# The six middle rounds in TensorE's program: a loop over pairs of rounds, or written out

## The chip, the cores and the metric

The kernel runs on one core of a Trainium2 chip. The metric is the device time of one launch in microseconds (us), as the median of several runs.

## What is computed

There are 4096 rows of 1024 numbers: 64 samples of 64 rows each. Two layers are added to `x`, one after the other. Cut to what matters:

```python
# layer 0: a 64x64 matrix for each sample mixes the sample's rows
y   = einsum('bct,bcd->bdt', x, weights0[cond])
h   = einsum('bnd,erd->bner', y, A0);  route = top-2 softmax of y @ W_gate.T
x   = x + (y @ W_base.T + b_base) + einsum('bner,eor->bno', h * route, B0)
# layer 1: a 1024x1024 adapter for each sample, then low rank
z   = einsum('bsi,boi->bso', x, weight1[adapter])
out = x + 2 * einsum('bshr,hor,bsh->bso', z @ A1, B1, 8 * softmax(z @ Wr.T + br))
```

Everything is float32. The kernel reaches nearly that accuracy by splitting both factors of a product into a high and a low part and adding three products.

## The kernel before

**Preparation.** In the first 84 us TensorE folds the adapter matrices of layer 1 with `A1` and `Wr` into matrices of 1024 x 136 (`fold`), with one turn of a loop for each adapter that is in use. They go to a DRAM buffer `folded`. The first rows are mixed (`mix`).

**Rounds.** After that the work goes in eight rounds (`ROUNDS = 8`) of 512 rows. In round r TensorE's program (`iteration`, lines 404 to 443) does layer 0 of round r, layer 1 of round r-1 and the mixing of round r+1:

- `gates` (L349, L351): 64 products, alternating 272 and 136 columns, into `mix_ps`, `low_ps` and `out_ps`.
- eight steps of `base` (L316 to L318, 12 products of 512 columns each), and after each step a `make_low` (L384, 8 products of 272 columns) for one sample of round r-1. `make_low` number i waits until the matrix of that sample has landed in slot i % 3 of `adapter`.
- `delta`, eight more steps of `base` with `mix` (L336) and `make_out` between them, `delta` again, and a last `make_out`.

TensorE executes in program order. Round 0 stands by itself, then come rounds 1 to 6, then round 7, whose second half of rows has code of its own. Rounds 1 to 6 are a loop of three turns with two rounds in each turn (L459 to L461):

```python
with pe.Fori(0, (ROUNDS - 2) // 2) as q:
    for r in (1, 2):
        iteration(q, r)
```

So turn 0 is rounds 1 and 2, turn 1 is rounds 3 and 4, turn 2 is rounds 5 and 6, and the program branches back twice: before round 3 and before round 5. In the loop, the value that a semaphore must reach is worked out from `q` in a register (`at`).

**The other engines** have the same loop of pairs in programs of their own, and the change leaves these alone. In each round, SyncE issues the loads of the next round's `x_rows` and `wc` (L236, L243), the two loads of 1 MB into `xT` (L254), and then the stores of the round before (L261), in this order. GpSimd loads the folded matrix of one sample (1.1 MB, L869) into a slot of `adapter` as soon as TensorE's `make_low` three samples before has finished with that slot (`low_done`). VectorE and ScalarE split and copy what TensorE has made.

Of the kernel before, what the change touches and what calls it, by code (L numbers as in the profile page):

```python
# [24 lines left out]
ROUNDS = TOKENS // T  # L25
# [20 lines left out]
def build(nc, x, x_turned, cond_ids, adapter_ids, w_cond, w0, g0, bias, b0, w1, ag1, b1, br, folded, out):  # L46
    with ExitStack() as ctx:
# [152 lines left out]
        def at(q, r, per, n=0):  # L200

            return 2 * per * q + (per * r + n)
# [111 lines left out]
        def _(pe):  # L314
# [14 lines left out]
            def mix(q, r, k):  # L329
                if k == 0:  # L330
                    pe.wait_ge(x_landed, at(q, r, 16 * TILES, 16 * TILES))
                    pe.wait_ge(wc_landed, at(q, r, 16 * PER, 16 * PER))
                if k >= 2:
                    pe.wait_ge(yT_lo_done, at(q, r, KC, k - 1))
                for t in range(TILES):
                    mm = pe.matmul(mix_ps[k % 2][:, t * P:(t + 1) * P], x_rows[:, t, k * P:(k + 1) * P], wc[:, t, :],  # L336
                                   start=True, stop=True, skip_group_check=True)
                mm.then_inc(yT_done, 1)

            def gates(q, r):  # L340
                for t in range(TILES):
                    tile = slice(t * P, (t + 1) * P)
                    if t >= 2 and (r >= 1 or not isinstance(q, int)):
                        pe.wait_ge(final_done, at(q, r - 2, KC, 2 * KC - 1 + t - 2))
                    for k in range(KC):
                        if t == 0 and k in (0, KC - 1):

                            pe.wait_ge(yT_lo_done, at(q, r, KC, KC - 1 if k == 0 else KC))
                        pe.matmul(hg_banks[t][:, 0:2 * HG], yT[:, 0, k, tile], g_hl[:, k, :, :].rearrange("p h n -> p (h n)"),  # L349
                                  start=(k == 0), stop=False, skip_group_check=True)  # L350
                        mm = pe.matmul(hg_banks[t][:, 0:HG], yT[:, 1, k, tile], g_hl[:, k, 0, :],  # L351
                                       start=False, stop=(k == KC - 1), skip_group_check=True)
                    mm.then_inc(hg_done, 1)

            def base(q, r, half, k, toks=ALL):
                bank = ALL if toks == ALL else A
                for n in range(4):
                    if k == 0:

                        if half == 1:  # L360
                            pe.wait_ge(x1_done, at(q, r + (toks == B), KC, n + 1))
                        elif toks == B:
                            pe.wait_ge(x1_done, at(q, r, KC, HALF + n + 1))
                        elif half == 0 and (r >= 1 or not isinstance(q, int)):
                            pe.wait_ge(x1_done, at(q, r - 1, KC, HALF + n + 1))
                    cols = slice((HALF * half + n) * P, (HALF * half + n + 1) * P)
                    product(base_ps[n][:, bank], w_hi[:, k, cols], w_lo[:, k, cols], yT[:, 0, k, toks],
                            yT[:, 1, k, toks], k == 0, False)

            def delta(half, toks=ALL):  # L370
                bank = ALL if toks == ALL else A
                for n in range(4):
                    cols = slice((HALF * half + n) * P, (HALF * half + n + 1) * P)
                    product(base_ps[n][:, bank], b0_hi[:, cols], b0_lo[:, cols], hwT[:, 0, toks], hwT[:, 1, toks],
                            False, True).then_inc(main_done, 1)

            def make_low(q, r, i, banks):
                pe.wait_ge(adapter_landed[i % SLOTS], 16 * at(q, r, (3, 3, 2)[i % SLOTS], i // SLOTS + 1))
                pe.wait_ge(x1T_lo_done, at(q, r, 2 * PER, 2 * i + 2))
                if i >= 2:  # L380
                    pe.wait_ge(lg_done, at(q, r, PER, i - 1))
                bank = banks[i % 2]
                for k in range(KC):
                    mm = pe.matmul(bank[:, 0:2 * HG], x1T[:, i % 2, k, :, :].rearrange("p h n -> p (h n)"),  # L384
                                   adapter[:, i % SLOTS, k, :, :].rearrange("p h n -> p (h n)"),
                                   start=(k == 0), stop=(k == KC - 1))
                mm.then_inc(low_done, 1)

            def turn_hw(q, r):
                pe.wait_ge(route_step, at(q, r, ROUTE_STEPS, ROUTE_STEPS))  # L390
                for t in range(TILES):
                    mm = pe.transpose(mix_ps[0][:, t * P:(t + 1) * P], rows[:, t, :], identity[:, :])
                mm.then_inc(hwT_done, 1)

            def turn_lw(q, r, tiles=range(TILES)):
                pe.wait_ge(score_step, at(q, r, SCORE_STEPS, SCORE_STEPS))
                for t in tiles:
                    mm = pe.transpose(low_ps[:, t * P:(t + 1) * P], rows[:, t, :], identity[:, :])
                mm.then_inc(lwT_done, 1)

            def make_out(q, r, n, bank, free, toks=ALL):
                if n == 0:
                    pe.wait_ge(lwT_lo_done, at(q, r, 1, 1))
                if free:
                    pe.wait_ge(final_done, at(q, r, KC, KC + free))
                cols = slice(n * P, (n + 1) * P)
                product(bank, b1_hi[:, cols], b1_lo[:, cols], lwT[:, 0, toks], lwT[:, 1, toks], True, True
                        ).then_inc(out_done, 1)

            def iteration(q, r, l1=True, ahead=True, toks=ALL):  # L410
                first = isinstance(q, int) and r == 0
                if first:
                    pe.wait_ge(g_split, 1)
                gates(q, r)
                for k in range(KC):
                    if first:
                        pe.wait_ge(side_lo, 1 + k)
                    base(q, r, 0, k, toks)
                    if l1:
                        if k < 2:  # L420
                            pe.wait_ge(hg_copied, at(q, r, TILES, TILES))
                        make_low(q, r - 1, k, low_banks)
                    if k == 5:
                        turn_hw(q, r)
                pe.wait_ge(hwT_lo_done, at(q, r, 1, 1))
                if first:
                    pe.wait_ge(side_lo, B0_SPLIT)
                delta(0, toks)
                for k in range(KC):
                    if first:  # L430
                        pe.wait_ge(side_lo, HALF1 + k // 2 + 1)
                    base(q, r, 1, k, toks)
                    if ahead:
                        mix(q, r + 1, k)
                    if l1 and k == 1:
                        turn_lw(q, r - 1)
                    if l1 and k >= 2:
                        make_out(q, r - 1, k - 2, out_ps[:, :], k - 2)
                if l1:
                    make_out(q, r - 1, KC - 2, low_ps[:, :], 0)  # L440
                delta(1, toks)
                if l1:
                    make_out(q, r - 1, KC - 1, out_ps[:, :], KC - 2)
# [12 lines left out]
                mix(0, 0, k)  # L456
            iteration(0, 0, l1=False)
            pe.wait_ge(side_lo, SIDES)
            with pe.Fori(0, (ROUNDS - 2) // 2) as q:  # L459
                for r in (1, 2):  # L460
                    iteration(q, r)  # L461
            last = ROUNDS - 1
            iteration(0, last, ahead=False, toks=A)

            for k in range(KC):
# [481 lines left out]
```

## Time and profile before

| | |
|---|---|
| median of 3 runs | 754.27 us (751.4 to 755.64) |
| the profiled execution: its own time | 755.48 us |
| its span in the profile | 753.8 us |
| TensorE busy | 723.9 us, 96% of the span |
| VectorE, ScalarE, GpSimd busy | 339.9, 113.6 and 57.9 us |
| DMA engines | mean 207 GB/s |

The profiled execution has its own time of 755.48 us beside a span of 753.8 us; 1.7 us lie around the span. "Idle" of an engine is the time between the end of one of its instructions and the start of the next. Matmuls overlap and their ends are modelled, so a distance from start to start is also used. The rounds begin with the first product of `gates`, at 160.75, 239.57, 320.16, 401.25, 482.58, 563.65 and 642.93 us for rounds 1 to 7. PEclk is the granted clock of TensorE, 1.00 for 2.4 GHz and 0.50 for 1.2 GHz.

### The profile page before, as it was taken

Reading aid. Unit: us, or ns where it says so; the run is one execution under the profiler, and the core shown is the slowest. Engines: PE = TensorE matmul, PEld = TensorE weight load, DVE = VectorE, ACT = ScalarE, POOL = GpSimd, SP = SyncE. Lnnn points to the kernel's source line nnn. Section 1 sums busy time; section 2 is a strip of 40 time slices with the busy share of each in tenths; the row PEclk is TensorE's granted clock in tenths of the full one; section 3 lists DMA queues with packets and bytes.
Section 4 is the critical chain, followed back from the end, with each engine's and each line's share of the span. In section 5 each row is a group of like instructions: output and inputs, shape, how many; then the busy total and the mean of one; then the engine's idle time right before and its main releaser. Section 6 shows DMA issues by size and latency. Waiting matters only on the chain.

```text
span 753.8 us, 12433 instructions
## 1 busy us (share of the span) xinstructions
PE 723.9 (96%) x4424; PEld 646.1 (86%) x4424; DVE 339.9 (45%) x900; ACT 113.6 (15%) x309; POOL 57.9 (8%) x115
## 2 busy tenths in 40 slices
PE   8999899999999999999999999899999999989984
PEld 8999887898888888797889888888889888989983
DVE  2000295145625553455426452455345443764544
ACT  1222300112111111101111211111111111111110
POOL 1222300001000110001000100011000000010100
PEclk9999999999999999999999999999999999999996
DMA  7899992038603882178514951467218831793622
GB/s 279 324 415 377 399 395 87 1 118 343 242 32 116 311 294 98 57 244 312 178 57 173 394 193 48 170 266 266 98 57 289 311 133 56 257 338 155 242 76 95
DMA packets 38708, 156.30 MB, mean 207 GB/s; under 512 B 8836, under 2 KB 11908, under 8 KB 28420
## 3 DMA queue, kind: packets, MB, share of 16 engines
q1 hardware_dynamic: 27714, 78.72, 28.0%
q0 software_dynamic: 9216, 71.31, 25.8%
q10 hardware_dynamic: 1730, 5.58, 1.8%
q8 instruction: 36, 0.59, 0.3%
q14 instruction: 12, 0.10, 0.0%
HBM read 133.24 MB, written 22.35 MB: 206 GB/s over the span
## 4 chain that ended last, share of the span: by engine, by line
PE 86%; DMA 5%; DVE 4%; issue 2%; SPq 2%; ACT 0%; POOLq 0%; DVEq 0%
PE base_ps L316 16%; PE base_ps L317 16%; PE base_ps L318 16%; PE base_ps L325 8%; PE mix_ps L336 7%; DMA adapter<-folded 4%; PE low_ps L384 4%; PE out_ps L384 4%; PE mix_ps L349 3%; PE out_ps L316 2%; PE out_ps L317 2%; PE out_ps L318 2%; DVE w_lo L629 1%; PE low_ps L349 1%; PE out_ps L349 1%
## 5 line engine op out<-in xcount | busy, mean ns | idle before, releaser
L316 PE MATMUL base_ps<-yT,w_hi 128*128 128x512 f32 (+1 forms) x576 | 214.5, 372 | 1.3 <-DVE xT L749 1.1
L318 PE MATMUL base_ps<-yT,w_hi 128*128 128x512 f32 (+1 forms) x576 | 211.5, 367 | 0.0
L317 PE MATMUL base_ps<-yT,w_lo 128*128 128x512 f32 (+1 forms) x576 | 211.4, 367 | 0.0
L633 DVE TENSOR_TENSOR yT<-mix_ps,yT 128x512 fp32r<-128x512 f32 x64 | 44.2, 691 | 240.0 <-ACT yT L515 239.8
L316 PEld LDWEIGHTS base_ps<-yT,w_hi 128*128 128x128 f32 x576 | 108.5, 188 | 20.8 <-DVE xT L749 4.0
L318 PEld LDWEIGHTS base_ps<-yT,w_hi 128*128 128x128 f32 x576 | 108.5, 188 | 18.1
L317 PEld LDWEIGHTS base_ps<-yT,w_lo 128*128 128x128 f32 x576 | 108.6, 188 | 15.5
L869 POOL DMA_DIRECT2D adapter<-folded x64 | 34.1, 532 | 606.2 <-PE low_ps L384 505.9
L645 DVE TENSOR_TENSOR x1T<-xT,x1T 128x256 fp32r<-128x256 f32 x128 | 48.3, 419 | 66.6 <-ACT x1T L523 66.6
L325 PE MATMUL base_ps<-ag_raw,stage 128*128 128x136 f32 x640 | 74.7, 279 | 2.3 <-issue 1.3
L325 PEld LDWEIGHTS base_ps<-ag_raw,stage 128*128 128x128 f32 x640 | 74.3, 190 | 2.8 <-issue 1.5
L523 ACT CAST x1T<-xT 128x256 fp32r<-128x256 f32 x128 | 44.7, 403 | 189.1 <-PE low_ps L384 63.6
L336 PEld LDWEIGHTS mix_ps<-wc,x_rows 128*128 128x128 f32 x512 | 66.0, 191 | 7.3 <-DVE yT L633 2.2
L515 ACT CAST yT<-mix_ps 128x512 fp32r<-128x512 f32 x64 | 37.5, 587 | 213.6 <-PE mix_ps L336 213.6
L336 PE MATMUL mix_ps<-wc,x_rows 128*128 128x128 f32 x512 | 67.1, 275 | 2.1 <-DVE yT L633 1.6
L749 DVE SCALAR_TENSOR_TENSOR xT<-base_ps,bias_cols,xT 128x512 f32<-128x512 f32 (+1 forms) x72 | 44.7, 683 | 8.0 <-PE base_ps L318 7.8
L755 DVE TENSOR_TENSOR xT<-xT,out_ps 128x512 f32<-128x512 f32 (+1 forms) x53 | 34.9, 659 | 9.2 <-PE out_ps L318 9.2
L384 PEld LDWEIGHTS low_ps<-adapter,x1T 128*128 128x128 f32 x240 | 33.0, 188 | 6.3 <-issue 3.1
L384 PE MATMUL low_ps<-adapter,x1T 128*128 128x272 f32 x240 | 35.2, 289 | 3.2 <-DMA adapter<-folded 3.2
L349 PE MATMUL mix_ps<-g_hl,yT 128*128 128x272 f32 x128 | 32.6, 346 | 4.1 <-issue 3.5
L384 PEld LDWEIGHTS out_ps<-adapter,x1T 128*128 128x128 f32 x240 | 33.2, 188 | 2.8 <-DVE lg L699 0.6
L384 PE MATMUL out_ps<-adapter,x1T 128*128 128x272 f32 x240 | 35.1, 288 | 0.2 <-DMA adapter<-folded 0.2
(126 smaller groups left out, 724.2 us busy)
## 6 DMA issues: line engine op xcount, KB each, us to landing
adapter<-folded POOLq DMA_DIRECT2D x64, 1088.0 KB, 7.0
stage<-in_w SPq DMA_DIRECT2D x40, 512.0 KB, 7.9
x_rows<-in_x SPq DMA_DIRECT2D x32, 512.0 KB, 6.0
xT<-in_x_turned SPq DMA_DIRECT2D x16, 1024.0 KB, 7.2
out<-xT SPq DMA_DIRECT2D x28, 512.0 KB, 2.7
folded<-adapter ACTq DMA_DIRECT2D x10, 544.0 KB, 6.9
w_raw<-in_w SPq DMA_DIRECT2D x8, 256.0 KB, 8.1
w_raw<-in_w SPq DMA_DIRECT2D x4, 512.0 KB, 12.0
```

The source lines that it names most:

```text
L316: pe.matmul(dst, st_hi, mv_lo, start=start, stop=False, skip_group_check=True)
L317: pe.matmul(dst, st_lo, mv_hi, start=False, stop=False, skip_group_check=True)
L318: return pe.matmul(dst, st_hi, mv_hi, start=False, stop=stop, skip_group_check=True)
L325: mm = pe.matmul(base_ps[c % BANKS][:, 0:HG], stage[:, c, oc * P:(oc + 1) * P], ag1_raw[:, oc, :], start=(oc == 0), stop=(oc == KC - 1))
L336: mm = pe.matmul(mix_ps[k % 2][:, t * P:(t + 1) * P], x_rows[:, t, k * P:(k + 1) * P], wc[:, t, :], start=True, stop=True, skip_group_chec ...
L349: pe.matmul(hg_banks[t][:, 0:2 * HG], yT[:, 0, k, tile], g_hl[:, k, :, :].rearrange("p h n -> p (h n)"), start=(k == 0), stop=False, skip_ ...
L384: mm = pe.matmul(bank[:, 0:2 * HG], x1T[:, i % 2, k, :, :].rearrange("p h n -> p (h n)"), adapter[:, i % SLOTS, k, :, :].rearrange("p h n ...
L515: act.copy(yT[:, 0, k, :], mix_ps[k % 2][:, :]).then_inc(yT_hi_done, 1)
L523: act.copy(x1T[:, i % 2, p * HALF:(p + 1) * HALF, 0, :], xT[:, half_of(r, p), :, i * CH:(i + 1) * CH]).then_inc(x1T_hi_done, 1)
L633: dve.tensor_tensor(yT[:, 1, k, :], mix_ps[k % 2][:, :], yT[:, 0, k, :], ALU.subtract).then_inc(yT_lo_done, 1)
L645: dve.tensor_tensor(x1T[:, i % 2, half, 1, :], xT[:, half_of(r, p), :, i * CH:(i + 1) * CH], x1T[:, i % 2, half, 0, :], ALU.subtract).then ...
L749: dve.scalar_tensor_tensor(row, base_ps[n % HALF][:, bank], bias_cols[:, n:n + 1], row, ALU.add, ALU.add).then_inc(x1_done, 1)
```

## The change

TensorE's loop over pairs of rounds is gone. A Python loop calls `iteration` for rounds 1 to 6 with `q = 0`, so that all six stand one behind the other in TensorE's program:

```diff
             pe.wait_ge(side_lo, SIDES)
-            with pe.Fori(0, (ROUNDS - 2) // 2) as q:
-                for r in (1, 2):
-                    iteration(q, r)
             last = ROUNDS - 1
+            for r in range(1, last):
+                iteration(0, r)
             iteration(0, last, ahead=False, toks=A)
```

The matrix products, their order and their operands stay as they are. The values that semaphores must reach are now constants. The programs of the other four engines are unchanged.

On TensorE, at the entry of the loop (end of round 0, start of round 1), the program was:

```order
L318 MATMUL base_ps<-hwT,b_hi 128x512
L459 UNCONDITIONAL_BRANCH
L459 ISA
L349 MATMUL mix_ps<-g_hl,yT 128x272
L351 MATMUL mix_ps<-g_hl,yT 128x136
```

The branch and the register instruction at L459 are gone; the first product of round 1 now follows the last one of round 0 directly.

On TensorE, at the end of the loop's body, before:

```order
L316 MATMUL out_ps<-lwT,b_hi 128x512
L317 MATMUL out_ps<-lwT,b_lo 128x512
L318 MATMUL out_ps<-lwT,b_hi 128x512
L459 REGISTER_ALU
L459 COMPARE_AND_BRANCH
L349 MATMUL mix_ps<-g_hl,yT 128x272
L351 MATMUL mix_ps<-g_hl,yT 128x136
```

and at the end of round 2 now:

```order
L316 MATMUL out_ps<-lwT,b_hi 128x512
L317 MATMUL out_ps<-lwT,b_lo 128x512
L318 MATMUL out_ps<-lwT,b_hi 128x512
L349 MATMUL mix_ps<-g_hl,yT 128x272
L351 MATMUL mix_ps<-g_hl,yT 128x136
```

In the first listing the branch goes back to the start of round 1's code for rounds 3 and 5, and the products below it are those of round 7. In the second the products below are those of round 3; nothing stands between the rounds. TensorE's written program grows from 1616 such rows to 2834, and 51 of its 59 register operations are gone.

## Rows read from the trace of the kernel before

**Rows 1.** The page, its busy times (TensorE) and its DMA queues (instruction fetches).
```profile
PE 723.9 (96%) x4424; PEld 646.1 (86%) x4424; DVE 339.9 (45%) x900; ACT 113.6 (15%) x309; POOL 57.9 (8%) x115
...
q8 instruction: 36, 0.59, 0.3%
```

**Rows 2.** TensorE's waits from 160 to 645 us: total, times, longest.
```profile
PE mix_ps L349 <- issue: 3.5, 2, 1.9
PE low_ps L384 <- DMA adapter<-folded: 1.9, 3, 1.5
PE mix_ps L351 <- issue: 0.2, 1, 0.2
```

**Rows 3.** Timeline of TensorE, round 1 into 2: start, duration, instruction.
```profile
239.34 0.39 PE L318 MATMUL out_ps<-lwT,b_hi 128*128 128x512 f32 x1
239.57 0.28 PE L349 MATMUL mix_ps<-g_hl,yT 128*128 128x272 f32 x1
```

**Rows 4.** The same, at the two branches back (rounds 2 into 3, 4 into 5).
```profile
318.15 0.39 PE L318 MATMUL out_ps<-lwT,b_hi 128*128 128x512 f32 x1
320.16 0.39 PE L349 MATMUL mix_ps<-g_hl,yT 128*128 128x272 f32 x1 [1.63 <-issue]
...
323.29 0.34 PE L349 MATMUL mix_ps<-g_hl,yT 128*128 128x272 f32 x1
323.85 0.22 PE L351 MATMUL mix_ps<-g_hl,yT 128*128 128x136 f32 x1 [0.22 <-issue]
...
480.28 0.39 PE L318 MATMUL out_ps<-lwT,b_hi 128*128 128x512 f32 x1
482.58 0.39 PE L349 MATMUL mix_ps<-g_hl,yT 128*128 128x272 f32 x1 [1.91 <-issue]
```

**Rows 5.** Instruction queue in the DMA view of 316.5 to 317, then 480 to 480.5.
```profile
q8 instruction: 1, 0.02, 21.2%
...
q8 instruction: 1, 0.02, 12.0%
```

**Rows 6.** Instruction queue in the DMA view of the whole round 1, then round 3.
```profile
q8 instruction: 4, 0.07, 0.3%
...
q8 instruction: 5, 0.08, 0.4%
```

**Rows 7.** Busy times by stretch, rounds 1, 3, 4, 5; third from last: granted clock.
```profile
160.75:239.57 78.82, 78.79 (x442) 68.48 (x440) 39.28 (x104) 11.72 (x28) 4.23 (x8) 1.00 0.50 183
...
320.16:401.25 81.09, 79.34 (x440) 68.62 (x441) 37.87 (x101) 10.59 (x25) 4.23 (x8) 1.00 0.53 190
401.25:480.28 79.03, 78.80 (x440) 68.23 (x439) 38.81 (x102) 11.71 (x28) 4.24 (x8) 1.00 0.53 194
482.58:563.65 81.07, 80.82 (x441) 70.15 (x441) 37.88 (x101) 10.39 (x24) 4.24 (x8) 0.98 0.52 190
```

**Rows 8.** The same view around the second branch back, and after the first.
```profile
482.00:484.00 2.00, 1.42 (x11) 1.43 (x12) 0.00 (x0) 0.50 (x2) 0.00 (x0) 0.98 0.69 266
484.00:486.00 2.00, 2.00 (x11) 2.00 (x11) 0.75 (x3) 0.00 (x0) 0.00 (x0) 0.50 0.91 324
486.00:488.00 2.00, 2.00 (x13) 2.00 (x13) 0.36 (x2) 0.00 (x0) 0.00 (x0) 0.66 1.07 313
...
322.00:324.00 2.00, 1.78 (x16) 1.68 (x16) 1.11 (x3) 0.00 (x0) 0.00 (x0) 1.00 0.92 279
```

**Rows 9.** Timeline of TensorE, `make_low` that waited, rounds 3 and 4.
```profile
347.66 0.39 PE L384 MATMUL low_ps<-adapter,x1T 128*128 128x272 f32 x1 [1.49 <-DMA adapter<-folded]
...
426.97 0.36 PE L384 MATMUL low_ps<-adapter,x1T 128*128 128x272 f32 x1 [0.20 <-DMA adapter<-folded]
```

**Rows 10.** Round 3: SyncE's `xT` loads, then the chain of waits.
```profile
334.89 0.87 SPq L254 DMA_DIRECT2D xT<-in_x_turned  x2
...
336.51 10.93 DMA adapter<-folded
```

**Rows 11.** Round 4: SyncE's `xT` loads, GpSimd's adapter load and its landing.
```profile
416.31 0.90 SPq L254 DMA_DIRECT2D xT<-in_x_turned  x2
...
417.11 0.54 POOL L869 DMA_DIRECT2D adapter<-folded  x1 [3.22 <-PE out_ps L384]
...
DMA to landing us min/median/max: 9.6/9.6/9.6
```

## The prediction, made before the changed kernel was run

> **What bounds the kernel now.** I read the busy times first: TensorE works for 723.9 us, 96% of the span, and no other engine comes to half of it [rows 1]. So only what TensorE executes and where it stands still counts. Next I read its waits over rounds 1 to 6, the stretch that the change touches: 3.5 us in two waits before L349 and 0.2 us before L351, all put down to "issue", that is to nothing that another engine or a transfer did, and 1.9 us in three waits for folded matrices [rows 2]. Then the timeline says where. Between rounds 1 and 2, where the program just runs on, the first product of `gates` starts 0.23 us after the last product before it [rows 3]. At the two branches back it starts 2.01 us (318.15 to 320.16) and 2.30 us (480.28 to 482.58) after [rows 4]. The reader should see that the same pair of instructions stands in all three places and that only the branch differs.
>
> The cause is in the instruction queue. A block of 0.02 MB is fetched there in an ordinary round about once in 20 us: four in round 1, whose TensorE had no gap [rows 6, 7]. One of them starts just before each long gap, at about 317 and 480 us [rows 5], which fits a sequencer that reaches the branch a little ahead of the array and must fetch the code it jumps to. Last come the rounds themselves: round 1 lasts 78.82 us, round 4 79.03, but rounds 3 and 5, those behind a branch, 81.09 and 81.07 [rows 7]. So each branch is followed by an excess of some 2.3 us beyond its own gap, and this has to be accounted for too.
>
> **The change part by part.**
>
> 1. *The two taken branches go.* The start-to-start distances shrink to the 0.23 us of an uninterrupted round: 2.01 - 0.23 = 1.78 and 2.30 - 0.23 = 2.07, together **3.85 us**, all on TensorE, all on the path. The entry of the loop and its exit cost nothing now that I could take away: all the "issue" waits of this stretch are the three already named [rows 2].
>
> 2. *A second, short halt behind the first branch goes.* L351 at 323.85 starts 0.56 us after its forerunner at 323.29 [rows 4], with 0.22 us shown idle. I take the idle time, **0.2 us**; the upper bound is some 0.4, the lower 0.
>
> 3. *The clock.* 2 us behind the second gap the granted clock falls to 0.50 (1.2 GHz) and is back at 1.00 by 488 us. The clock missing over three stretches of 2 us is 0.02 + 0.50 + 0.34 = 0.86 of one stretch, so 1.7 us of work was lost [rows 8]. That explains most of round 5's excess. What TensorE did before it fell was to stand still for 1.91 us with no other halt near. Behind the first gap the clock stayed at 1.00 [rows 8]. Rounds 1, 3 and 4, which do the same work, stay at 1.00 too [rows 7]. I take the whole **1.7 us** as gone with the gap; the lower bound is 0, if the fall was chance or not in the median run.
>
> 4. *The late matrix of round 3.* TensorE stood 1.49 us for it, against 0.20 in round 4 [rows 9]. In round 3 GpSimd issued the load 1.62 us behind SyncE's two loads into `xT` (334.89, 336.51), and it took 10.93 us [rows 10]; in round 4 the distance is 0.80 us and the load took 9.6 [rows 11]. SyncE's time does not hang on TensorE's gap, because its stores and loads were released before the gap; GpSimd's load does. With the gap gone, round 3's load is issued 1.78 us earlier, at 334.7, just ahead of the `xT` loads. Its nearest row is round 4's, so I take 1.49 - 0.20 = **1.3 us**. Bounds: 1.5 if it no longer waits, and -1.3 for each round in which the wait turns as long as in round 3.
>
> 5. *Register operations and waits.* 51 register operations of the loop's body are gone. TensorE ran through all of round 1 in 78.82 us with 78.79 us busy [rows 7], so its sequencer's extra work was hidden behind the array: **0**. The products hide it, and the cover stays. If it went, the whole saving would be that idle time, 0.03 us.
>
> 6. *More code to fetch.* The executed products are the same, 4424 [rows 1], so about the same number of blocks is fetched: the 36 less the few that a jump fetches again. Round 3 executes the code of round 1 a second time and still fetched five blocks [rows 6], so nothing was kept for reuse that the change would lose. Straight code between blocks shows no halt in round 1: **0**; the bound above is in the last rival.
>
> Sum: 3.85 + 0.2 + 1.7 + 1.3 = 7.05 us. Against the profiled execution's own 755.48 us this gives 748.4. That execution is 1.2 us above the median of the runs, 754.27, and the runs spread over 4 us, so the median run may lack part of term 3. I keep **748.5 us**, 0.8% below the median before. What is next late after the change: the folded matrices of rounds 3 to 6 by some 0.2 us each, hardly worth a name.
>
> A rule about the branches can be set beside term 1. The Trainium skill (Runtime: NRT & Kernel Launch, Instruction fetch mechanics) says that prefetch is purely sequential and that a taken branch outside the fetched window must fetch its target first. By that rule the trace agrees: halts of 1.63 and 1.91 us, each with a block fetched, and none elsewhere. Another page, Advanced Engine Details and Errata of the Trainium skill, section Control Flow Timing, gives some 108 ns for a compare-and-branch. By that figure alone term 1 would be an estimated 0.2 us and the kernel would stay at 754; the two gaps speak against it.
>
> **The rivals.**
>
> *A. Only the gaps go.* The clock falls elsewhere or fell by chance, and the matrices stay as late. For: the clock stayed up behind the first gap. Against: between 160 and 645 us it fell once, behind the longer gap. Only terms 1 and 2 are left: 754.27 - 4.05 = 750.2 us.
>
> *B. The transfers take it back.* Terms 1 to 3 give 5.75 us, but SyncE keeps its loop, and its loads now stand differently against TensorE. If round 3 keeps its long wait and rounds 4, 5 and 6 each wait 1.3 us more, 3.9 us are given back: 754.27 - 5.75 + 3.9 = 752.4 us. For: one step of 0.8 us between two issues made 1.3 us [rows 10, 11]. Against: the change brings round 3's distance nearer to that of the others, and rounds 4 and 6 have it anyway.
>
> *C. The halt does not belong to the branch.* The fetch that came late is one of a block in any place where the DMA engines are loaded, and the written-out code meets the same at two block boundaries. Then nothing is gained: 754.3 us. Against: four blocks in round 1 without a halt [rows 6]. The 108 ns of the Trainium skill (Advanced Engine Details and Errata, Control Flow Timing) would lead here too.
>
> *D. Slower: straight code stalls at its blocks.* Between 160 and 643 us some 24 blocks are needed; a boundary where the block is late would cost about what the branches cost, 1.8 to 2.1 us. Against the full gain of 7 us it decides from the fourth such boundary on, and is slower by over 0.5% from the sixth; with all 24 it is 754.3 - 7.1 + 24 x 1.9 = 793 us. For: at 323.85 the second block behind a branch was late once [rows 4]. Against: rounds 1 and 4 ran with 0.03 and 0.23 us idle [rows 7], in code of just this form.
>
> **How the numbers follow.** About 0.5%, or 3.8 us, is what a measurement of this kernel can tell from no change; "faster" therefore means below 750.5 us. The forecast has a chance of 0.58, A 0.18, B 0.12, C 0.08 and D 0.04. A's 750.2 lies at the edge: I give 0.14 of it to faster and 0.04 to no change. Faster: 0.58 + 0.14 = 0.72. Same: 0.04 + 0.12 + 0.08 = 0.24. Slower: 0.04. For the range: the lower end is the forecast less the small waits for matrices of rounds 4 to 6 (0.2 each) and the 1.2 us by which the profiled run differs from the median, and another microsecond of the spread of the runs, 745.5. The upper end takes in A and reaches to B's 752.4: 752.5. C and D stay outside, with half of B's own spread and a little below the lower end, some 2 in 10.
>
> **What would show it.** In the profile after, the first L349 of rounds 3 and 5 starts 0.2 to 0.3 us after the last L318, and the waits for "issue" between 160 and 640 us are gone (term 1, 2). Every round from 1 to 6 lasts 78.8 to 79.3 us with the clock at 1.00 (term 3). Round 3's `make_low` waits 0.2 us or less (term 4). The instruction queue moves some 34 to 36 blocks (term 6). I am wrong if halts for "issue" stand at other places inside rounds, if the clock still falls between 160 and 640 us, or if the waits for `adapter` sum to more than 1.9 us.

## The result and the profile after

The changed kernel takes 748.43 us (median of 8 runs, 747.44 to 751.06). The kernel before, run beside it, takes 754.83 us (8 runs, 751.4 to 758.61). The ratio is 0.9913 with a 95% interval of 0.9894 to 0.9932: 0.9% faster, where 748.5 us and 0.8% were forecast. The profiled execution took 748.9 us with a span of 747.2 us. The agreement of the total is better than that of its parts, as the rounds show below. Three runs, two of the kernel before and one of e4, took 1040 to 1855 us, far from all others of the same kernels, and are left out of all ratios and counts.

The page after, TensorE and the instruction queue, as in [rows 1]:

```profile
PE 722.1 (97%) x4424; PEld 645.1 (86%) x4424; DVE 339.8 (45%) x900; ACT 113.6 (15%) x309; POOL 57.9 (8%) x115
...
q8 instruction: 32, 0.52, 0.3%
```

These are the same 4424 products with 1.8 us less of busy time (round 5, in which the clock fell before, went from 80.82 to 79.05), and 32 blocks of code instead of 36. TensorE's waits from 160 to 640 us, which answer to [rows 2]:

```profile
PE out_ps L384 <- DMA adapter<-folded: 2.3, 2, 1.4
PE low_ps L384 <- DMA adapter<-folded: 0.2, 1, 0.2
```

No wait for "issue" is left, but those for folded matrices have grown from 2.1 us (the 1.9 of [rows 2] and one of 0.2 us before an `out_ps` product, which [rows 2] leaves out) to 2.5 us. The timeline at the starts of rounds 3 and 5, as in [rows 4]:

```profile
319.04 0.39 PE L318 MATMUL out_ps<-lwT,b_hi 128*128 128x512 f32 x1
319.26 0.28 PE L349 MATMUL mix_ps<-g_hl,yT 128*128 128x272 f32 x1
...
478.17 0.39 PE L318 MATMUL out_ps<-lwT,b_hi 128*128 128x512 f32 x1
478.40 0.28 PE L349 MATMUL mix_ps<-g_hl,yT 128*128 128x272 f32 x1
```

Both distances are 0.22 to 0.23 us, as between rounds 1 and 2 [rows 3]. The busy times of rounds 1, 3, 4 and 5 (third column from the end: granted clock), as in [rows 7], and of the stretch behind the former second branch, as in [rows 8]:

```profile
161.36:240.24 78.88, 78.85 (x442) 68.49 (x440) 39.27 (x104) 11.71 (x28) 4.23 (x8) 1.00 0.51 184
319.26:399.33 80.07, 79.08 (x441) 68.42 (x440) 39.04 (x103) 11.71 (x28) 4.23 (x8) 1.00 0.53 192
399.33:478.40 79.07, 79.05 (x442) 68.42 (x440) 39.04 (x103) 11.71 (x28) 4.24 (x8) 1.00 0.53 195
478.40:558.83 80.43, 79.05 (x441) 68.42 (x440) 39.03 (x103) 11.72 (x28) 4.24 (x8) 1.00 0.52 192
...
480.00:482.00 2.00, 2.00 (x19) 2.00 (x18) 1.11 (x3) 0.39 (x2) 0.00 (x0) 1.00 0.76 277
482.00:484.00 2.00, 2.00 (x19) 2.00 (x19) 1.11 (x3) 0.00 (x0) 0.00 (x0) 1.00 0.95 307
```

The clock stays at 1.00 (2.4 GHz). But rounds 3 and 5 still last 1.2 and 1.6 us longer than the 78.85 us of an undisturbed round, and their idle time is 1.0 and 1.4 us. The longest wait stands before the same kind of instruction as in [rows 9], for the matrix of a later sample:

```profile
509.02 0.39 PE L384 MATMUL out_ps<-adapter,x1T 128*128 128x272 f32 x1 [1.35 <-DMA adapter<-folded]
```

From the start of round 1 to that of round 7 it was 482.18 us before and is 476.81 after: 5.4 us come from the stretch that the change touches. The rest of the span differs by 1.2 us (0.6 more ahead of round 1, 1.8 less from round 7 on), where the program is the same. In all the profiles taken the part from round 7 on takes between 108.5 and 111.5 us, so the 1.8 us lie within what it varies by.

### The profile page after: what moved, and what is told of

It is laid out like the page before. It is cut to its first block, busy times and chain, and to the rows that moved or that the text cites. A ratio compares the mean times of both kernels' runs of the same rounds, so it can differ in the third digit from the quotient of the medians.

```text
span 747.2 us, 12250 instructions
## 1 busy us (share of the span) xinstructions
PE 722.1 (97%) x4424; PEld 645.1 (86%) x4424; DVE 339.8 (45%) x900; ACT 113.6 (15%) x309; POOL 57.9 (8%) x115
## 4 chain that ended last, share of the span: by engine, by line
PE 87%; DMA 6%; DVE 4%; issue 1%; ACT 0%; POOL 0%; POOLq 0%; DVEq 0%
PE base_ps L316 16%; PE base_ps L317 16%; PE base_ps L318 16%; PE base_ps L325 10%; PE mix_ps L336 7%; DMA adapter<-folded 6%; PE low_ps L384 4%; PE out_ps L384 4%; PE mix_ps L349 3%; PE out_ps L316 2%; PE out_ps L317 2%; PE out_ps L318 2%; DVE w_lo L628 1%; PE out_ps L349 1%; PE low_ps L349 1%
## 5 line engine op out<-in xcount | busy, mean ns | idle before, releaser
L316 PEld LDWEIGHTS base_ps<-yT,w_hi 128*128 128x128 f32 x576 | 108.5, 188 | 20.9 <-DVE xT L748 4.0
L318 PEld LDWEIGHTS base_ps<-yT,w_hi 128*128 128x128 f32 x576 | 108.5, 188 | 18.1
L325 PEld LDWEIGHTS base_ps<-ag_raw,stage 128*128 128x128 f32 x640 | 75.9, 193 | 2.2 <-issue 2.2
L349 PE MATMUL mix_ps<-g_hl,yT 128*128 128x272 f32 x128 | 30.7, 333 | 0.6 <-DVE yT L632 0.6
```

The source lines that it names most:

```text
L316: pe.matmul(dst, st_hi, mv_lo, start=start, stop=False, skip_group_check=True)
L318: return pe.matmul(dst, st_hi, mv_hi, start=False, stop=stop, skip_group_check=True)
L325: mm = pe.matmul(base_ps[c % BANKS][:, 0:HG], stage[:, c, oc * P:(oc + 1) * P], ag1_raw[:, oc, :], start=(oc == 0), stop=(oc == KC - 1))
```

## The experiments

Each kernel ran beside the kernel before, three batches in all; the kernel before took 755.47, 756.4 and 756.12 us in them. Ratios are to it.

**e1, one pair of rounds taken out of the loop.**

```diff
-            with pe.Fori(0, (ROUNDS - 2) // 2) as q:
+            for r in (1, 2):
+                iteration(0, r)
+            with pe.Fori(1, (ROUNDS - 2) // 2) as q:
                 for r in (1, 2):
                     iteration(q, r)
```

> Rounds 1 and 2 are written out, rounds 3 to 6 stay a loop of two turns, so TensorE branches back once (before round 5) instead of twice. Fetch theory (a taken branch back must fetch its target before TensorE goes on): round 3 starts 0.23 us after the last product before it, round 5 still 2.0 to 2.3 us after; of the change's 6.4 us about 2 to 4 are gained, so 751 to 753 us. Rival (the halts come from register operations or something that the loop does once as a whole): both gaps stay or both go.

Measured: 752.56 us, ratio 0.9976 (0.9955 to 0.9997). Timeline of TensorE at the starts of rounds 3 and 5, then busy times by stretch behind the second:

```profile
318.30 0.39 PE L318 MATMUL out_ps<-lwT,b_hi 128*128 128x512 f32 x1
318.52 0.28 PE L349 MATMUL mix_ps<-g_hl,yT 128*128 128x272 f32 x1
...
478.08 0.39 PE L318 MATMUL out_ps<-lwT,b_hi 128*128 128x512 f32 x1
480.30 0.39 PE L349 MATMUL mix_ps<-g_hl,yT 128*128 128x272 f32 x1 [1.83 <-issue]
...
480.00:482.00 2.00, 1.70 (x11) 1.70 (x11) 0.00 (x0) 0.30 (x1) 0.00 (x0) 0.75 0.89 289
482.00:484.00 2.00, 2.00 (x11) 2.00 (x10) 0.44 (x2) 0.00 (x0) 0.00 (x0) 0.50 0.88 320
```

The halt is where a branch is taken back over two rounds and nowhere else, and the clock falls behind it once more.

**e2, a branch back to the instruction just before.** In the written-out program, at the starts of rounds 3 and 5:

```diff
             for r in range(1, last):
+                if r in (3, 5):
+                    with pe.Fori(0, 2):
+                        pe.wait_ge(const_set, 5)
                 iteration(0, r)
```

> All six rounds written out, and at the starts of rounds 3 and 5 a loop of two turns around nothing but a wait that is long fulfilled, so TensorE again takes one branch back at each of the two places, but to an instruction just before it. Fetch theory: the target is at hand, no gap beyond 0.3 us at either place, time equal to the changed kernel's within 0.5 us, 748 to 749. Rival (a taken branch costs TensorE 1.8 us wherever it goes): gaps of 2.0 us and more return at both places, 752 us or more.

Measured: 747.28 us, ratio 0.9897 (0.9871 to 0.9924). The timeline at the start of round 5:

```profile
476.56 0.39 PE L318 MATMUL out_ps<-lwT,b_hi 128*128 128x512 f32 x1
476.79 0.28 PE L349 MATMUL mix_ps<-g_hl,yT 128*128 128x272 f32 x1
```

The queue of TensorE has the branch instructions themselves, with min/median/max in ns. First the loop over pairs of the kernel before (one branch falls through, two are taken), then the near loops of e2 (two fall through, two are taken):

```profile
L459 PEldq COMPARE_BRANCH  x3: 83/4146/4427, 315.9 to 640.4; - x3
...
L462 PEldq COMPARE_BRANCH  x4: 76/146/219, 316.1 to 474.7; - x4
```

A taken branch as such takes 0.22 us at most. It begins over 2 us ahead of the product that follows it, while earlier products still run, and so adds nothing. Those back over two rounds take 4.15 and 4.43 us; the first, from 315.85 to 320.00, ends just before the first product of round 3 at 320.16. The cost hangs on where the branch leads.

**e8, a loop over single rounds.** Six turns of one round, five branches back over half as much code; `at` in TensorE's program gets a stride of one round:

```diff
+            def at(q, r, per, n=0):
+                return per * q + (per * r + n)
...
-            for r in range(1, last):
-                iteration(0, r)
+            with pe.Fori(0, ROUNDS - 2) as q:
+                iteration(q, 1)
```

> TensorE's six middle rounds as a loop of six turns with one round in each: the program branches back five times, over half as much code as before the change (some 900 instructions). Fetch theory without any room for old code: a gap of about 2.0 us from start to start at all five branches, 5 x 1.8 = 9 us more than the changed kernel, and the clock falls behind the longer ones: 757 to 762 us, slower than the kernel before. Rival (the fetched code of one round is still held, and only the two-round loop was too long): no gaps, 748 to 749 us like the changed kernel.

Measured: 747.82 us, ratio 0.9906 (0.9876 to 0.9935). My theory as I had put it fell here, and its rival held. TensorE at the start of round 3, its only waits from 160 to 640 us, the queues that moved anything from 240 to 636 us, and its six branches (the last falls through):

```profile
318.68 0.39 PE L321 MATMUL out_ps<-lwT,b_hi 128*128 128x512 f32 x1
318.90 0.28 PE L352 MATMUL mix_ps<-g_hl,yT 128*128 128x272 f32 x1
...
PE low_ps L387 <- DMA adapter<-folded: 1.2, 2, 0.7
...
q0 software_dynamic: 5760, 44.57, 30.7%
q1 hardware_dynamic: 10367, 32.05, 21.6%
q14 instruction: 4, 0.03, 0.0%
...
L463 PEldq COMPARE_BRANCH  x6: 76/208/223, 237.2 to 634.1; - x6
```

Queue q8, which brought four or five blocks in each round before [rows 6], has no row at all in 396 us. The five taken branches last 0.21 to 0.22 us. So the code of one round is held and run again without a fetch, and that of two rounds is not. The Trainium skill (Runtime: NRT & Kernel Launch, Instruction fetch mechanics) gives TensorE room for 2048 instructions. The loop over pairs has about 1840 in a turn (440 products and 440 weight loads in each round, and some 75 others) and halted, the loop over single rounds about half of that and did not. By that figure alone the loop over pairs would fit too, and no run here shows why it does not; where between the two the limit lies was not tried. The same section speaks of a window of only two blocks, outside of which a taken branch must fetch; the four blocks that e8 used again say otherwise, and the measurement decides.

**e3, SyncE written out too.** The same edit as the change, in SyncE's program on top of it.

> The changed kernel with SyncE's loop written out as well. Theory (what is left of the waits for folded matrices in rounds 3 and 5, 0.96 and 1.35 us, comes from SyncE's own branch back, which makes its four x_rows issues 0.8 to 1.0 us longer and its xT loads 1.0 to 1.3 us late): the xT loads of rounds 3 and 5 are issued 15.1 to 15.3 us into the round as in rounds 2, 4 and 6, the two waits fall to about 0.2 us, 1.9 us less than the changed kernel: 746.5 us. Rival (the waits belong to TensorE's position against the loads): they stay, 748.4 us.

Measured: 749.15 us, ratio 0.9929 (0.9901 to 0.9957). The waits from 160 to 640 us:

```profile
PE low_ps L383 <- DMA adapter<-folded: 0.8, 3, 0.4
```

In this profile rounds 3 and 5 have no wait left, and 0.2 to 0.4 us stand in rounds 2, 4 and 6 instead. Part of my reason holds: the `x_rows` issues of rounds 3 and 5 begin 1.56 us into the round, as in all others, where those of the changed kernel begin 2.41 and 2.36 us into it (1.91 in rounds 4 and 6), and the `xT` loads follow 14.9 and 14.4 us into the round instead of 16.3 and 16.4. But round 3's four `x_rows` issues still took 2.88 us with no loop in SyncE's program, and in e2, with SyncE's loop, they took 2.06, so their length does not come from that branch. And the time is that of the changed kernel: SyncE's loop shifts the loads, but taking it away gains nothing that can be measured.

**e5, the changed kernel again.**

> The changed kernel once more, as the measure for the runs beside it: 748 to 749 us, no gap between rounds 1 and 7, waits for folded matrices of 0.2 to 1.4 us at places that may differ from those of the first profile (349 and 509 us).

Measured: 749.14 us (747.51 to 751.67), ratio 0.9923 (0.9895 to 0.9952). The waits were 0.50, 0.93 and 0.43 us, at 349, 508 and 584 us: the same rounds as in the first profile.

**e6, the `xT` loads ahead of the `wc` loads,** in SyncE's program, on top of the change:

```diff
                     load_x(q, r + 1)
-                    load_wc(q, r + 1)
                 if l0:
                     load_xT(q, r, 0)
                     load_xT(q, r, 1)
+                if ahead:
+                    load_wc(q, r + 1)
```

> The changed kernel, but SyncE issues the two xT loads ahead of the eight small wc loads instead of behind them, about 10 us earlier in the round. Theory (the waits for folded matrices in rounds 3 to 6 come from the 2 MB of xT running at the same time as GpSimd's second or third load of the round): the xT loads are done before GpSimd's first load, no make_low of rounds 1 to 6 waits, each of these rounds lasts 78.8 to 78.9 us, 2 to 3 us less than the changed kernel: 746 us. Rival (the folded loads are late by themselves, 1.1 MB in 3.8 us each): the waits stay and the time is the changed kernel's, 748.4 us.

Measured: 745.42 us (744.80 to 745.73), ratio 0.9869 (0.9845 to 0.9894). Busy times of rounds 3, 5 and 6:

```profile
318.94:397.77 78.83, 78.80 (x442) 68.47 (x440) 39.04 (x103) 11.72 (x28) 4.23 (x8) 1.00 0.55 195
...
476.60:555.42 78.82, 78.79 (x441) 68.49 (x440) 39.03 (x103) 11.72 (x28) 4.25 (x8) 1.00 0.55 195
555.42:634.21 78.79, 78.77 (x442) 68.48 (x440) 39.05 (x103) 11.72 (x28) 4.24 (x8) 1.00 0.56 195
```

Every round is undisturbed, with 0.02 to 0.03 us idle. The runs lie within 1 us of each other, where those of the changed kernel spread over 4. That the overlap made the spread is not shown: e10, with the same early loads, spreads over 3.7 us, and e2, without them, over 1.4.

**e9, the same on the kernel before,** with TensorE's loop over pairs kept.

> The kernel before, TensorE's loop over pairs kept, with only SyncE's xT loads moved ahead of the wc loads. Theory (the two costs are separate): no make_low waits in rounds 1 to 6, but the halts for issue at the starts of rounds 3 and 5 stay at 2.0 to 2.3 us from start to start, and the clock falls behind one of them in many runs: 2 to 3 us less than before, 752 to 753 us. Rival (the late matrices were a consequence of the branch): less than 1 us gained.

Measured: 750.59 us, ratio 0.9940 (0.9922 to 0.9959). The waits from 160 to 640 us:

```profile
PE mix_ps L350 <- issue: 2.8, 2, 1.7
PE mix_ps L352 <- issue: 0.3, 1, 0.3
```

The matrices are on time and the halts stay, though shorter (1.56 and 2.06 us from start to start). The two costs are separate. The gain of some 5.5 us is more than the 2 to 3 I expected. In the profiles rounds 1 to 6 are 5.4 us shorter than before (476.79 against 482.18): 0.7 us from the shorter halts, 1.7 from the clock, which did not fall between 160 and 640 us in this profile, and the remaining 3.0 from the matrices. Why the halts are shorter is open.

**e10, a loop over single rounds with the early `xT` loads.**

> TensorE's loop of six turns of one round, and the xT loads ahead of the wc loads. Theory (code of one round is held, so the short loop costs nothing and its missing block fetches no longer get in the way of SyncE's issues): 745 to 746 us, the same as the written-out program with the early xT loads (745.4). Rival (the short loop's branch costs something that the matrix waits hid): 5 gaps of some tenths, 746.5 us or more.

Measured: 745.76 us (744.14 to 747.82), ratio 0.9868 (0.9848 to 0.9888), the same as e6 within the intervals, and no wait of TensorE at all from 160 to 640 us. These two beat both kernels, and e10 fetches 14 blocks of TensorE's code where e6 fetches 32.

**e4 and e7, halts without a branch.** The written-out program, and TensorE waits before rounds 3 and 5 for VectorE's last operation, to which one memset (e4) or two (e7, whose edit stands here) are added. The memsets overwrite `rows` and `lg`, which are no longer needed there.

```diff
+                if r in (3, 5):
+                    pe.wait_ge(halt_over, r // 2)
                 iteration(0, r)
...
+                dve.memset(rows[:, :, :], 0.0)
+                dve.memset(lg[:, :, 0:HR], 0.0).then_inc(halt_over, 1)
```

> The changed kernel with a halt of TensorE before rounds 3 and 5 that has no branch: it waits for VectorE's last operation of the round before, a memset of the tile rows that VectorE does once in each pair of rounds (about 0.5 us, 1.6 to 2.0 us of idle time on TensorE). Clock theory (the stop of nearly 2 us is what lets the granted clock fall): behind at least one of the two halts PEclk shows 0.50 for some us, and the time is above the changed kernel's by more than the two halts, 752 us and more. Rival (the fall at 484 us was chance or needs the branch): the clock stays at 1.00 from 160 to 640 us and the time rises by the halts alone, 3 to 4 us.

> As the halt without a branch, with a second memset in VectorE (the tile lg), so that TensorE stands for about 2.0 to 2.2 us instead of 1.59 before rounds 3 and 5. Clock theory, now with a length (1.83 us and 1.91 us of idle time were followed by a fall of the clock, 1.59 and 1.63 us were not): the clock falls to 0.50 behind one or both halts, 1.7 us of work lost each, 754 us or more. Rival (the fall needs the branch, or something else at 480 us): PEclk 1.00 from 160 to 640 us, 752 us.

Measured: e4 751.23 us, ratio 0.9947 (0.9928 to 0.9965), two halts of 1.59 us; e7 752.73 us, ratio 0.9968 (0.9947 to 0.9988), two halts of 2.13 us. In neither profile did the clock fall between 160 and 640 us. Going by the profiles alone the rival would stand, but a profile is one execution; the mean granted clock is known for each, and is counted below.

**e11, five halts.** As e7, with the early `xT` loads, at the starts of rounds 2 to 6.

> The written-out program with the early xT loads, and a halt without a branch of about 2.1 us (waiting for two memsets of VectorE) at the start of each of rounds 2 to 6. Clock theory (a stop of about 2 us now and then lets the clock fall, with no branch needed): at least one fall to 0.50 between 235 and 570 us in the profile, mean granted clock of the runs 0.980 to 0.986, time 745.4 + 5 x 2.3 + falls = 757 us and 1.7 us for each fall, 758 to 762. Rival (halts alone don't do it): PEclk 1.00 over the whole stretch, mean clock 0.988 to 0.991, 757 us.

Measured: 765.26 us, ratio 1.0138 (1.0110 to 1.0165). Busy times by stretch, around the halts before rounds 4 and 6:

```profile
402.00:404.00 2.00, 0.49 (x3) 0.07 (x1) 1.95 (x4) 1.00 (x4) 0.00 (x0) 1.00 0.00 0
404.00:406.00 2.00, 1.38 (x7) 1.38 (x8) 0.51 (x2) 0.32 (x2) 0.00 (x0) 0.74 0.78 262
406.00:408.00 2.00, 2.00 (x11) 2.00 (x10) 0.00 (x0) 0.00 (x0) 0.00 (x0) 0.50 0.92 317
408.00:410.00 2.00, 2.00 (x18) 2.00 (x17) 1.11 (x3) 0.00 (x0) 0.00 (x0) 0.90 1.05 371
...
566.00:568.00 2.00, 0.52 (x3) 0.10 (x1) 1.94 (x4) 0.97 (x4) 0.00 (x0) 1.00 0.00 0
570.00:572.00 2.00, 2.00 (x11) 2.00 (x10) 0.00 (x0) 0.00 (x0) 0.00 (x0) 0.50 0.91 285
```

Two of five halts were followed by a fall to 0.50 (1.2 GHz), with no branch in sight. The median lies above the 758 to 762 us that I expected, and the mean clock of four of the six runs lies below the expected 0.980 to 0.986 (0.971 to 0.979): the profiled run, with 0.987, was the mildest. One fall costs 0.26 + 0.50 + 0.10 = 0.86 of a stretch of 2 us, 1.7 us, as in [rows 8]; on the mean clock of a run that is 0.0023. One run's mean does not tell whether the clock fell in the rounds, because the clock also falls in the rest of the program: in the 13 profiles that costs between 6.8 and 10.8 us. So only counts over many runs say something:

| TensorE's halts between rounds 1 and 7 | kernels | runs with a mean clock below 0.987 |
|---|---|---|
| none for the program or by hand | changed, e2, e3, e5, e6, e8, e10 | 6 of 43 |
| two of 1.59 us | e4 | 2 of 11 |
| two of 2.13 us, no branch | e7 | 9 of 12 |
| five of 2.13 us, no branch | e11 | 5 of 6 |
| one or two by a far branch (1.2 to 1.9 us) | before, e1, e9 | 43 of 67 |

The two halts of 1.59 us of e4 can't be told from none, as its rival had it; those of 2.13 us can.

## Why the prediction was right, and where it was not

- **Term 1, the two branches: right.** 3.85 us were forecast, and both distances shrank to 0.22 to 0.23 us. e1 and e2 tie the halt to a taken branch that leads far, e8 to code that is not held, and rival C is out. The branches back began at 315.85 and 477.99 us and took 4.15 and 4.43 us; the fetch of a block began 1.0 and 2.1 us behind their starts and ended before theirs.
- **Term 2, the second halt: right.** No such wait is left; from start to start it had been 0.39 us more than usual, near the upper bound.
- **Term 3, the clock: right.** 1.7 us were forecast, and the clock stayed at 1.00. That a halt is enough, with no branch, is shown by the profile of e11; the counts of e7 support it. It is a matter of chance in each run, as the table shows. Over many runs it is still worth about the 1.7 us of one profile: the mean clock is 0.9866 over the 49 runs of the kernel before that ran beside the experiments and 0.9889 over the 43 in the table's first row, 0.0023 apart with a standard error of 0.0005. The one fall of the one profile could not show that; that the two agree was luck.
- **Term 4, the late matrix: wrong.** The step that failed is "Its nearest row is round 4's, so I take 1.49 - 0.20 = 1.3 us". Without terms 1 to 3 (here 3.85 + 0.39 + 1.72 us) rounds 1 to 6 lasted 3.4 us longer than six times 78.81 before, and 4.0 us longer after: 0.6 us lost instead of 1.3 gained. Round 3 gained 0.6 us, and round 5, which had no place in the sum, lost 1.1. "SyncE's time does not hang on TensorE's gap" held in round 3: its `xT` loads were issued 174.14 us after the start of round 1 before and 174.15 after. GpSimd's load came 2.0 us earlier, and so stood 0.39 us ahead of them, not 0.80 behind as in round 4. The next one, 3.6 us behind them, was the late one now:

```profile
335.12 0.53 POOL L868 DMA_DIRECT2D adapter<-folded  x1 [3.21 <-PE out_ps L384]
335.51 1.11 SPq L254 DMA_DIRECT2D xT<-in_x_turned  x2
339.11 0.54 POOL L868 DMA_DIRECT2D adapter<-folded  x1 [3.45 <-PE low_ps L384]
```

  In round 5 TensorE came 4.8 us earlier than before, counted from the start of round 1, and the `xT` loads only 1.8 us, so they fell 16.4 us into the round instead of 13.4: the halts had given SyncE a lead. In e4, whose halts have no branch, it is the same, with `xT` 13.6 us into rounds 3 and 5. Rival B's mechanism is real, at a smaller price than I gave it. What I had also missed is that SyncE's own issues are not constant. The `x_rows` issues of rounds 5 and 4 after, the instruction queue from 482 to 482.5 us, SyncE's `xT` loads of round 5 and the folded matrix that was late (landing last):

```profile
480.76 3.15 SPq L236 DMA_DIRECT2D x_rows<-in_x  x4
...
401.24 2.10 SPq L236 DMA_DIRECT2D x_rows<-in_x  x4
...
q8 instruction: 1, 0.02, 15.9%
...
494.80 0.90 SPq L254 DMA_DIRECT2D xT<-in_x_turned  x2
...
498.24 0.53 POOL L868 DMA_DIRECT2D adapter<-folded  x1 [3.45 <-PE low_ps L384]
...
DMA to landing us min/median/max: 10.7/10.7/10.7
```

  The `xT` loads came 16.4 us into round 5, against 15.1 us in round 4, so one folded load was under way when they began and the next was issued 3.4 us behind them; that one took 10.7 us and was late. One of TensorE's code blocks was fetched from 482.3 us on, in the midst of the slow issues; in round 3, before and after, one began within 0.2 us of their start. In e8, which fetches no blocks there, all these issues took 2.06 to 2.26 us. That a fetch slows the issues is an inference from such coincidences: no run moved a fetch alone, and in e2 one that began 0.4 us ahead of round 3's issues did them no harm (2.06 us); and as e8 still waited 0.70 and 0.51 us for matrices, it is not the whole cause. That the overlap with `xT` is the cause of the waits is shown by e6.
- **Term 5, register operations: right.** Round 1 lasted 78.82 before and 78.88 us after, and e10, which works its waits out in registers as before, has rounds of 78.79 to 78.84 us.
- **Term 6, code to fetch: right as to its cost, wrong in a reason.** No wait for "issue" stands at any block boundary in rounds 1 to 6, so rival D is out. But "nothing was kept for reuse" holds for a loop of two rounds alone; e8 reuses all of one round. The blocks went from 36 to 32, two below what I had given.
- **The total: luck in part.** The touched stretch gave 5.4 us, not 7.05; term 4 alone makes 1.9 us of the difference, and 0.2 came back in term 2. The profiled execution's 748.9 us still came near the sum, because 1.2 us were gained outside that stretch, where the program is the same and no term stood. The sum was also taken from the slower 755.48 us of the profiled execution, and 748.5 kept for the median; from the median of 754.27 it would have given 747.2. And the lower end of the range, added up as the text has it, is 745.7, not 745.5.

## What to carry to other kernels

Look at the start of each turn of a loop for a wait that nothing in the profile explains, and at the instruction queue beside it: if blocks are fetched on the second turn, the body does not fit, and a shorter body is as good as writing the loop out (e8, e10). A halt of some 2 us on TensorE can cost nearly twice its length when the clock falls behind it. And once the halts are gone, ask which transfers now run side by side: moving one pair of loads (e6) gave 3.7 us more.

## What was not expected of the hardware

TensorE's code of one round, four blocks of 0.02 MB, was run six times with no fetch between 240 and 636 us, while that of two rounds was fetched anew in each turn. A fall of the granted clock is not certain behind a stop: behind two stops of 2.13 us 9 of 12 runs had a low mean clock, behind two of 1.59 us 2 of 11, with no stop 6 of 43. A taken branch of TensorE lasted 0.21 to 0.22 us where its target was held, and 4.15 and 4.43 us where it was not, of which 1.6 and 1.9 us reached the array. Four issues of SyncE that take 2.1 us took 3.15 us when a code block of TensorE was fetched in their midst; that the fetch did it is not shown.
